# A gated recurrence on one core: first plain products split by column half, the first sigmoids ahead of ScalarE's copies, a tile of their own for the last residuals

## The reference

```
Xz = X @ Wxz.T + bxz;  Xr = X @ Wxr.T + bxr;  Xh = X @ Wxh.T + bxh      (all steps)
Z = sigmoid(xz + H @ Whz.T + bhz)
R = sigmoid(xr + H @ Whr.T + bhr)
H_tilda = tanh(xh + R * H @ Whh.T + bhh)
H_new = Z * H + (1.0 - Z) * H_tilda                                     (512 times)
Y = H_new @ Whq.T + bhq
out = x + Y
```

## Time and profile before

| | us |
|---|---|
| median of 3 runs | 2113.72 (2111.3 to 2114.66) |
| the profiled execution's own time | 2110.0 |
| its span, first to last instruction | 2108.2 |
| TensorE busy | 2084.8 (99%) |
| VectorE, ScalarE, GpSimd busy | 1568.6, 1226.9, 885.1 |
| mean granted TensorE clock | 0.999 |

### The profile page before, as it was taken

How to read it: one execution, slowest core, us unless ns; L and a number is a source line. 1 busy time by engine, 2 the same in 40 slices (tenths; PEclk the granted TensorE clock), 3 DMA queues, 4 the chain that set the end, 5 groups by cost and what they waited for, 6 DMA issues and landing times.

```text
span 2108.2 us, 204973 instructions
## 1 busy us (share of the span) xinstructions
PE 2084.8 (99%) x88464; PEld 2069.1 (98%) x88464; DVE 1568.6 (74%) x9106; ACT 1226.9 (58%) x5994; POOL 885.1 (42%) x1830
## 2 busy tenths in 40 slices
PE   9899999999999999999999999999999999999997
PEld 7899999999999999999999999999999999999997
DVE  4777777777777777777777777777777777777776
ACT  2465566565556556665655565565656565655654
POOL 3344444444444444444444444444444444444431
PEclk9999999999999999999999999999999999999999
DMA  4010100000000101000000001000000000010000
GB/s 162 18 29 19 27 25 22 27 25 22 27 25 20 30 17 27 26 21 27 25 22 27 25 20 30 18 27 27 20 27 25 22 27 25 20 30 20 25 23 24
DMA packets 84285, 58.39 MB, mean 28 GB/s; under 512 B 9490, under 2 KB 75410, under 8 KB 83474
## 3 DMA queue, kind: packets, MB, share of 16 engines
q1 hardware_dynamic: 84240, 57.81, 9.2%
q10 hardware_dynamic: 4, 0.02, 0.0%
HBM read 41.01 MB, written 16.78 MB: 27 GB/s over the span
## 4 chain that ended last, share of the span: by engine, by line
PE 98%; DMA 1%; DVE 1%; issue 1%; ACT 0%; SPq 0%; DVEq 0%
PE u_bank L628 42%; PE v_bank L628 21%; PE y_bank L559 9%; PE d_bank L527 8%; PE b_bank L527 7%; PE a_bank L527 6%; PE c_bank L527 3%; DMA w_all<-in_w_x 0%; PE u_bank L544 0%; PE b_bank L544 0%; PE a_bank L544 0%; DVE pre_t L1052 0%; DVE scanned L1156 0%; PE c_bank L544 0%; DMA out<-y_io 0%
## 5 line engine op out<-in xcount | busy, mean ns | idle before, releaser
L1052 DVE STREAM_TRANSPOSE pre_t<-u_bank 128x32 f32<-128x32 f32 (+1 forms) x3072 | 455.6, 199 | 186.8 <-PE u_bank L628 144.7
L628 PE MATMUL u_bank<-wh,scanned 128*16 128x128 f32 (+1 forms) x16384 | 542.4, 273 | 11.0 <-DVE scanned L1156 7.4
L318 POOL TENSOR_TENSOR x_parts<-z_of 128x96 f32<-128x96 f32 x744 | 338.4, 458 | 506.3 <-DVE h_sums L1072 237.2
L628 PE MATMUL u_bank<-wh,reset_state 128*16 128x128 f32 (+1 forms) x16384 | 542.4, 273 | 2.5 <-DVE reset_state L1207 2.5
L628 PE MATMUL v_bank<-wh,scanned 128*16 128x128 f32 (+1 forms) x16384 | 542.2, 273 | 2.2 <-issue 2.2
L628 PEld LDWEIGHTS v_bank<-wh,scanned 128*16 128x16 f32 (+1 forms) x16384 | 455.0, 104 | 3.0 <-issue 2.9
L628 PEld LDWEIGHTS u_bank<-wh,scanned 128*16 128x16 f32 (+1 forms) x16384 | 428.0, 103 | 15.1 <-DVE scanned L1156 7.6
L628 PEld LDWEIGHTS u_bank<-wh,reset_state 128*16 128x16 f32 (+1 forms) x16384 | 428.0, 104 | 3.3 <-issue 2.3
L1040 ACT ACTIVATE scan_on<-pre_t 128x16 f32<-128x16 f32 (+1 forms) x1536 | 238.2, 219 | 296.0 <-DVE pre_t L1052 296.0
L318 POOL TENSOR_TENSOR z_of<-z_of 128x96 f32<-128x96 f32 x558 | 255.3, 457 | 261.7 <-DVE scan_on L1234 136.1
L1014 ACT ACTIVATE r_gate<-pre_t 128x16 f32<-128x16 f32 (+1 forms) x1536 | 234.8, 215 | 174.9 <-DVE pre_t L1052 167.4
(11 more groups left out here) (141 smaller groups left out, 2810.6 us busy)
## 6 DMA issues: line engine op xcount, KB each, us to landing
y_io<-in_x_res SPq DMA_DIRECT2D x256, 64.0 KB, 2.0
out<-y_io SPq DMA_DIRECT2D x256, 64.0 KB, 1.6
x_all<-in_x_t SPq DMA_DIRECT2D x62, 256.0 KB, 2.6
w_all<-in_w_x SPq DMA_DIRECT2D x2, 1536.0 KB, 7.8
wh<-in_w_hr SPq DMA_DIRECT2D x1, 1024.0 KB, 11.1
wh<-in_w_hz SPq DMA_DIRECT2D x1, 1024.0 KB, 14.5
wh<-in_w_hh SPq DMA_DIRECT2D x1, 1024.0 KB, 16.5
wq<-in_w_q SPq DMA_DIRECT2D x1, 1024.0 KB, 6.3
```

Source lines behind the costliest of these rows:

```text
L318: nc.gpsimd.tensor_tensor(*of, ALU.add).then_inc(made, 1)
L628: mm = nc.tensor.matmul(gate_rows(g, par, slice(Q * j, Q * j + rows)), of, wh[g][:, m, P * j:P * (j + 1)], start=False, stop=(m == G - 1), ...
L1052: nc.vector.transpose(flat(pre_t[g][:, a:b]), gate_part(g, par, a, b)).then_inc(done, 1)
```

## The change

1. The two first plain pairs are split. Columns 0 to 191 of pairs 0 and 1 (`part` 0) need only the first half of the weights and come first; the biases of `a_bank`, `c_bank` and `d_bank` follow; then columns 192 to 383 (`part` 1) behind a wait for the second half.
2. ScalarE calculates a sigmoid of something (the tile `sigmoid_first`, read by nobody) right behind its copy of the bias rows.
3. ScalarE's copies of q = 2 and 3 move from ahead of step 0's first sigmoid to ahead of step 1's, in front of the copy of q = 4.
4. VectorE's `w_t4` moves ahead of step 0's transposition of R.
5. The last two pairs' residuals have a tile `y_last` and are loaded at the start. At the end there is no load, and the additions and stores use that tile.

```
             load_res(0, 0)
             load_res(1, 1)
+            for par in range(2):
+                sp.dma_start(y_last[:, par], x_res[pairs - 2 + par]).then_inc(y_last_loaded[par], 16)
             turn_loop(sp, turn)
             for par in range(2):
-                sp.wait_ge(stored[par], 16 * (2 * turns - 1))
-                load_res(pairs - 2 + par, par)
-            for par in range(2):
-                store(pairs - 2 + par, par)
+                sp.wait_ge(y_added, pairs - 1 + par)
+                sp.dma_start(out[pairs - 2 + par], y_last[:, par]).then_inc(stored[par], 16)
...
-            def plain_to_gates(q):
+            def plain_to_gates(q, part):
                 par = q % 2
-                plain(q, lambda rows, lo, hi: u_bank[par][rows, lo:hi], 0, RH)
-                plain(q, lambda rows, lo, hi: v_bank[rows, P * par + lo - RH:P * par + hi - RH], RH, P)
+                lo, hi = ((0, HALF), (HALF, RH))[part]
+                plain(q, lambda rows, lo, hi: u_bank[par][rows, lo:hi], lo, hi - lo)
+                if part:
+                    plain(q, lambda rows, lo, hi: v_bank[rows, P * par + lo - RH:P * par + hi - RH], RH, P)
...
+            biases_to(b_bank, 0, COLS).then_inc(biases_in, 1)
+            biases_to(u_bank[0], 0, RH)
+            biases_to(u_bank[1], 0, RH)
+            biases_to(v_bank, RH, RH)
             pe.wait_ge(x_first_loaded, 16)
             pe.wait_ge(wx_loaded[0], 16)
+            plain_to_gates(0, 0)
+            plain_to_gates(1, 0)
+            for bank in (a_bank, c_bank, d_bank):
+                biases_to(bank, 0, COLS)
             pe.wait_ge(wx_loaded[1], 16)
-            plain_to_gates(0)
-            plain_to_gates(1)
+            plain_to_gates(0, 1)
+            plain_to_gates(1, 1)
...
-                        for q in {0: (2, 3), 1: (4,), 2: (5,), 3: (6,), 4: (7,)}.get(s8, ()):
+                        for q in {1: (2, 3, 4), 2: (5,), 3: (6,), 4: (7,)}.get(s8, ()):
                             keep_plain(q)
...
                     if first and s8 == 1:
+                        act.wait_ge(plain_out, 2)
                         for to in (a_bank, b_bank):
                             nc.scalar.copy(to[:, 0:COLS], bias_rows[:]).then_inc(bank_ready, 1)
...
             nc.scalar.copy(bias_rows[:], b_bank[:, 0:COLS]).then_inc(bias_ready, 1)
+            act.wait_ge(bias_ready, 1)
+            nc.scalar.activation(sigmoid_first[:], bias_rows[:, 0:B], ACT.Sigmoid)
             turn_loop(act, turn)
...
+                    if first and s8 == 0:
+                        w_t4(0)
+                        w_t4(1)
...
-                        if s8 == 0:
-                            w_t4(0)
-                            w_t4(1)
-                        elif s8 == 1:
+                        if s8 == 1:
...
             dve.wait_ge(y_projected, 1)
-            add_y(0, 2 * turns, a_bank[:, 0:P])
+            dve.wait_ge(y_last_loaded[0], 16)
+            nc.vector.tensor_tensor(y_last[:, 0, :], a_bank[:, 0:P], y_last[:, 0, :], ALU.add).then_inc(y_added, 1)
             dve.wait_ge(y_projected, 2)
-            add_y(1, 2 * turns, outputs(1))
+            dve.wait_ge(y_last_loaded[1], 16)
+            nc.vector.tensor_tensor(y_last[:, 1, :], outputs(1), y_last[:, 1, :], ALU.add).then_inc(y_added, 1)
```

More of the change, by code:

```diff
@@ L59, in gru @@
         bias_rows = sb("bias_rows", [P, COLS])
+        sigmoid_first = sb("sigmoid_first", [P, B])
         start_of = sb("start_of", [P, 4, 4 * BLOCK])
@@ L82, in gru @@
         y_io = sb("y_io", [P, 2, P])
+        y_last = sb("y_last", [P, 2, P])
         scanned = sb("scanned", [P, 2, G, 3 * B, 2])
@@ L164, in gru @@
         y_loaded = [sem("y_loaded0"), sem("y_loaded1")]
+        y_last_loaded = [sem("y_last_loaded0"), sem("y_last_loaded1")]
         y_projected = sem("y_projected")
@@ L779, in _, with biases_to @@
             pe.wait_ge(bias_loaded, 16)
-            for to, at, cols in ((b_bank, 0, COLS), (u_bank[0], 0, RH), (v_bank, RH, RH), (u_bank[1], 0, RH),
-                                 (a_bank, 0, COLS), (c_bank, 0, COLS), (d_bank, 0, COLS)):
+            def biases_to(to, at, cols):
                 for j in range(G):
@@ L784, in _ @@
                                           start=True, stop=True)
-                if to is b_bank:
-                    mm.then_inc(biases_in, 1)
+                return mm
+            biases_to(b_bank, 0, COLS).then_inc(biases_in, 1)
+            biases_to(u_bank[0], 0, RH)
+            biases_to(u_bank[1], 0, RH)
+            biases_to(v_bank, RH, RH)
             pe.wait_ge(x_first_loaded, 16)
             pe.wait_ge(wx_loaded[0], 16)
+            plain_to_gates(0, 0)
+            plain_to_gates(1, 0)
+            for bank in (a_bank, c_bank, d_bank):
+                biases_to(bank, 0, COLS)
             pe.wait_ge(wx_loaded[1], 16)
-            plain_to_gates(0)
-            plain_to_gates(1)
+            plain_to_gates(0, 1)
+            plain_to_gates(1, 1)
             pe.wait_ge(x_second_loaded, 16)
```

## The result

| | before | changed |
|---|---|---|
| median, us | 2110.64 (7 runs, 2109.46 to 2114.66) | 2104.3 (7 runs, 2103.18 to 2105.24) |
| ratio, 95% interval | | 0.9967 [0.9957, 0.9978] |
| the profiled execution: own time, span | 2110.0, 2108.2 | 2105.24, 2103.5 |

The change makes the kernel 6.3 us faster by the medians. The forecast was 5.75 us faster, but at 2108.0 us, with a range from 2105.2 up. The forecast made against the profiled execution, 2104.25, is within 0.1 us of the measured median.

The account below looks back on a forecast made before the run. TensorE was taken as the bound, busy 99%, with gains only in the first 50 and last 10 us. 2.4 + 1.7 + 1.45 + 0.2 = 5.75 us, taken from the median 2113.72, gave 2108.0 us; range 2105.2 to 2111.5.

Parts of the forecast that it names:

- The base: Level the forecast gain was subtracted from: median of three runs, 2113.72 us, instead of the profiled execution's 2110.0.
- The hole and the clock behind it: First step: TensorE's wait before gate H closes, 2.4 us; without it no low clock on the products behind, 1.7 us.
- rival C: Low clock from 28.6 to 32.5 us is in the profiled execution alone; 1.7 us of gain missing, 2109.7; chance 0.12.
- The end: Last addition no longer waits for a residual's load and starts at 2104.4 instead of 2105.86 us; gain 1.45 us.
- The start: Split first products: step 0's gate R at 18.5 us, gain 0.2 us; bounds 1.0 sooner to 1.5 later.
- the unfavourable end: Start's worst case: pace sinks again at the bias groups, another slow start of 0.6 us, gate R at 20.2 us.
- Rivals D: A later wait, as at 59.54 us, swallows the first step's 4.1 us; 2112.1 us; chance 0.09.
- E: Repeated part becomes slower because its code's place in memory moved and rounds wait for code; 2114 us or more; chance 0.05.

Follow-up runs that it names:

- end_only: The kernel before with only the last two pairs' residuals in their own tile, loaded at the start; 2109.53 us, ratio 0.9998 against the kernel before.
- no_table: The changed kernel without ScalarE's early unread sigmoid (`sigmoid_first`); 2104.66 us, ratio 0.9969 against the kernel before.

## Why the prediction was right or wrong

**The base: wrong, and the step that failed.** "That execution is 3.7 us below the median of the three runs ... I take the difference over to the median: 2108.0." The difference was right and the level wrong. The three runs happened to lie high in what over 80 runs of the kernel before gave, 2108.21 to 2114.66 with medians of 2110.63 to 2112.1; the profiled execution, 2110.0, was the better base. So the term of the sum that was mis-sized is the base, 2113.72 where seven runs give 2110.64; from there the forecast difference leads to 2104.9. The range added 2 us for a run's spread at either end, but nothing for a median of three runs, 3.4 us apart, being 3 us off.

**The hole and the clock behind it: right.** Forecast 2.4 and 1.7 us. Measured from gate R of step 0 on: the hole 2.5 us (9.93 - 7.40), the products behind it 1.7 us (5.15 - 3.47). Timed alone the step has -4.0 us. What the prediction attributed to three edits is due to one, the copies. And rival C was partly true: end_only has the hole without the low clock. "With no hole I expect no low clock" held for the first step only: two stretches of it stand elsewhere in the changed kernel's profile.

**The end: right.** 1.46 us in the profiles against 1.45, both in the changed kernel and in end_only; against the other profiles without edit 5 it is up to 2.3. Timed alone it can't be told from nothing.

**The start: mechanism half right, size within the bounds by luck.** Forecast gate R at 18.5, bounds 17.7 and 20.2; 19.00, 19.31 and 17.70 in three profiles of the changed kernel. The first products took the slow pace as said, but for all of the 64 records: 5.13 us in place of 4.3. The three bias groups took 2.07 us, near the lower bound of 1.9. The 128 records behind them were costed at 0.03 us each, 3.8 us, from 96 of before in 2.74 us; but 32 of those 96 had 192 columns (0.041 us each), which leaves 0.022 for the others. At full pace the 128 take 2.67 us. The clock fell behind the biases, as the unfavourable end had it, and cost 1.4 us where the prediction put 0.6, a figure that no row gives. These errors cancel to 0.5 us.

**Rivals D and E: not seen.** The waits of the first pass through the repeated part (0.75, 1.40, 1.40, 1.79, 0.68, 1.75 us before; 0.77, 0.94, 1.16, 1.30, 0.41, 2.00 after) moved along with the program and were 1.2 us shorter in sum, a gain that was in no term and that differs from one profile of a kernel to the next. The low clock from 74 us on hid more than that. The profile's 4.7 us so add up: 3.90 to the start of step 1, 1.1 by the later waits, 1.7 lost at the second low clock, 1.46 at the end. So the hole, the clock behind it and the end bear the forecast of 5.75 us; that the start, the later waits and the second low clock leave the medians' 6.3 us so near to it is luck.

## What to carry to other kernels

When one execution's profile and a median of three runs disagree by more than the effect, make the forecast as a difference and put the disagreement itself into the range. An instruction that waits for a late producer holds what needs nothing from it: moving two copies by one step gave the same as the three edits to the first step together. When a start is made faster, look at what arrives at its own time (here, as it seems, a block of code), for the gain can end there. And look for the low clock over the whole profile, not only where it was: it can come back behind another wait.

## What the runs showed of the hardware

- Stretches of some 3.4 us at the low clock (0.50 of 2.4 GHz, so 1.2 GHz) came in some executions of a kernel and not in others. Behind the hole of 2.17 us: in two of three profiles. Between 68 and 80 us: in eight of 18, each time within 0.8 us of the end of a wait of 1.73 to 2.30 us; in seven other profiles waits of 1.73 to 2.02 us had none behind them. So at these places it stood behind a wait of TensorE each time, and the wait did not bring it each time.
- In the changed kernel it also came while TensorE was never idle, 1.1 us behind 2.07 us of products with two rows; of the six profiles with three such groups behind the first products four had it.
- The first products ran at half pace although the profile prints a granted clock of 1.00 there: 0.080 us for a 192-column record at the start, 0.041 later. At the start the pace of the records tells the state, and the printed clock doesn't.
- Straight-line code seems not to be free at the start: in the nine profiles that have the wait TensorE resumed 2.4 to 2.8 us after a 16 KB block of instructions was on the queue, and that block's moment varied from 18.0 to 22.0 us. What sets it is open: later loads of gate H's weights did not bring it sooner.
- The load of ScalarE's function table doesn't wait with the sigmoid it belongs to: with nothing ahead of both it ran at 5.25 us and the sigmoid at 20.40 (no_table).
